# The expert output's running sum: VectorE's add moved to GpSimd, and the copy of the down weights moved ahead in two queues

## The reference, cut to what matters

```
x = x + xattn(layernorm(x), ctx)
h = layernorm(x)
cw = softmax(h @ w_router) * softmax(h @ w_gating / 0.1);  cw /= sum(cw) + 1e-9
for each expert e:  out += cw[:, e] * ((silu(h @ w_gate[e]) * (h @ w_up[e])) @ w_down[e])
x = x + out          # w_gate, w_up: 8 x 256 x 1024; w_down: 8 x 1024 x 256
```

## Time and profile before

| | us |
|---|---|
| median of 3 runs | 963.75 (963.47 to 965.87) |
| the profiled execution, by the device's time | 965.87 |
| its span, first to last instruction | 963.9 |
| PE busy | 959.1 |
| DVE busy | 541.0 |
| ACT busy | 615.3 |
| POOL busy | 642.4 |

### The profile page before, as it was taken

The page is one execution under the profiler, slowest core; times in us unless marked ns, Lnnn a source line. Parts: engine busy times, 40 slices in busy tenths (PEclk is TensorE's granted clock), DMA queues, the critical chain, the costliest instruction groups (busy, mean ns, idle before and its releaser), DMA issues.

```text
span 963.9 us, 14994 instructions
## 1 busy us (share of the span) xinstructions
PE 959.1 (100%) x5090; PEld 890.0 (92%) x5090; DVE 541.0 (56%) x1024; ACT 615.3 (64%) x1109; POOL 642.4 (67%) x536
## 2 busy tenths in 40 slices
PE   9999999999999999999999999999999999999998
PEld 7999899999999999999999999999999999999998
DVE  4998455455555655556555565555555555555564
ACT  6988556666666566666666566666666565666662
POOL 5899975956566665766565675667565656757564
DMA  7462412311001110111010110111100110112035
GB/s 194 141 157 82 126 60 72 112 46 60 23 23 44 42 64 22 45 41 42 23 44 23 42 63 23 45 41 42 45 23 22 43 61 23 45 42 67 14 53 139
DMA packets 73233, 55.85 MB, mean 58 GB/s; under 512 B 30244, under 2 KB 69485, under 8 KB 73158
## 3 DMA queue, kind: packets, MB, share of 16 engines
q1 hardware_dynamic: 73150, 54.91, 19.6%
q10 hardware_dynamic: 8, 0.00, 0.0%
HBM read 46.58 MB, written 6.48 MB: 55 GB/s over the span
## 4 chain that ended last, share of the span: by engine, by line
PE 97%; DVE 1%; DMA 1%; ACT 0%; issue 0%; SPq 0%; DVEq 0%; ACTq 0%
PE ps L355 95%; PE ps L1874 1%; DMA xf<-in_L_xattn_Wk 1%; PE ps L1910 0%; PE ps L1862 0%; PE ps L1927 0%; DVE early L1371 0%; ACT arena L892 0%; DVE xsacc L1562 0%; PE ps L1953 0%; PE ps L1820 0%; ACT xf L900 0%; ACT xf L892 0%; ACT early L879 0%; DVE ps L1553 0%
## 5 line engine op out<-in xcount | busy, mean ns | idle before, releaser
L355 PE MATMUL ps<-arena 128*128 128x448 f32 (+5 forms) x2064 | 388.3, 339 | 0.1
L355 PEld LDWEIGHTS ps<-arena 128*128 128x128 f32 (+2 forms) x2064 | 343.7, 187 | 21.0 <-DVE arena L366 0.4
L702 POOL TENSOR_TENSOR arena<-shared,arena 128x448 fp32r<-128x448 f32 x196 | 223.8, 1160 | 190.7 <-ACT arena L1107 186.8
L355 PE MATMUL ps<-xc_hi,w_hi 128*128 128x448 f32 x904 | 330.8, 366 | 0.1
L355 PE MATMUL ps<-xc_hi,w_lo 128*128 128x448 f32 x904 | 330.2, 365 | 0.0
L355 PE MATMUL ps<-xc_lo,w_hi 128*128 128x448 f32 x904 | 330.2, 365 | 0.0
L355 PEld LDWEIGHTS ps<-xc_hi,w_hi 128*128 128x128 f32 x904 | 169.8, 188 | 14.0 <-DVE ps L1496 0.5
L355 PEld LDWEIGHTS ps<-xc_hi,w_lo 128*128 128x128 f32 x904 | 169.8, 188 | 13.6
L355 PEld LDWEIGHTS ps<-xc_lo,w_hi 128*128 128x128 f32 x904 | 169.9, 188 | 13.1
L1107 ACT CAST arena<-shared 128x448 fp32r<-128x448 f32 x180 | 102.2, 568 | 108.4 <-DVE shared L1521 44.0
L1553 DVE TENSOR_TENSOR ps<-ps,xf 128x448 f32<-128x448 f32 x104 | 65.6, 631 | 146.3 <-PE ps L355 146.3
(11 more groups left out here) (171 smaller groups left out, 1068.1 us busy)
## 6 DMA issues: line engine op xcount, KB each, us to landing
early<-in_L_ffn_w_down SPq DMA_DIRECT2D x16, 512.0 KB, 3.9
xf<-cw_dram SPq DMA_DIRECT2D x16, 448.0 KB, 4.6
shared<-in_ctx SPq DMA_DIRECT2D x16, 336.0 KB
w_raw<-in_L_ffn_w_gate SPq DMA_DIRECT2D x17, 256.0 KB, 2.7
w_raw<-in_L_ffn_w_up SPq DMA_DIRECT2D x17, 256.0 KB, 3.1
early<-in_L_ffn_w_gate SPq DMA_DIRECT2D x15, 256.0 KB, 2.7
early<-in_L_ffn_w_up SPq DMA_DIRECT2D x15, 256.0 KB, 3.1
xsacc<-in_x SPq DMA_DIRECT2D x8, 224.0 KB, 6.1
```

The lines of the kernel that those rows point to most:

```text
L355: ins = nc.tensor.matmul(dst, w, m, start=first and i == 0, stop=last and i == len(passes) - 1, skip_group_check=onto)
L702: nc.gpsimd.tensor_tensor(h[:, 1, j, at:at + TC], tile, h[:, 0, j, at:at + TC].bitcast(fp32), ALU.subtract).then_inc(hid_lo_done, 1)
```

## The change

Groups 4 to 29 get their add from GpSimd. VectorE now multiplies from PSUM into one of two SBUF buffers (`weighed`, two slots of `xf`) and raises `weighed_done`; GpSimd's new `add_unit` adds the buffer to the accumulator and raises `unit_done`. TensorE's units and SP's loads of shares wait for `weighed_done` instead of `unit_done`. VectorE's multiply of unit u waits for GpSimd's add of unit u-2. From set 2 on, `high_down` stands ahead of `gate_seed` on ScalarE, and `low_down` is the first of the quad on GpSimd. In quads 5 and 63 `up_c22` goes behind two `add_rows`.

```diff
+        weighed = [xf[:, 4 + i, :] for i in range(2)]
@@ SP, load_cw
-                    sp.wait_ge(unit_done, UNITS * (HALVES * CP * e - 2 * CP + cp + 1))
+                    sp.wait_ge(weighed_done, UNITS * (HALVES * CP * e - 2 * CP + cp + 1))
@@ GpSimd
+            def add_unit(g, k):
+                if g < 2 * CP:
+                    return
+                u = UNITS * (g - CP) + k
+                pool.wait_ge(weighed_done, u + 1)
+                at_least(pool, unit_done, u - 2 * UNITS * CP + 1)
+                to = unit_at(g, k)
+                nc.gpsimd.tensor_tensor(to, to, weighed[u % 2], ALU.add).then_inc(unit_done, 1)
             def quad(n):
+                if turn == 2 and hn > 1:
+                    low_down(hn)
                 if n > PLAIN:
                     low_hidden(n - 1, HID21, g21, 0, TC)
-                if turn == 2:
-                    low_down(hn)
+                g = n // FPAIRS - 1
+                if n % FPAIRS and g in TURNED:
+                    add_unit(g, 0)
+                    add_unit(g, 1)
+                if n % FPAIRS == 0 and g - 1 in TURNED:
+                    add_unit(g - 1, 3)
...
+                if turn == 2 and hn == 1:
+                    low_down(hn)
                 if turn == 2 and hn + 1 < SETS:
                     sums_of_set(2 * hn + 3)
+                if n % FPAIRS and g in TURNED:
+                    add_unit(g, 2)
...
@@ ScalarE, quad
+                if turn == 2 and hn > 1:
+                    high_down(hn)
                 gate_seed(n)
...
-                if turn == 2:
+                if turn == 2 and hn == 1:
                     high_down(hn)
@@ VectorE, weigh
-                rows, to, share = ps_unit[u % 2], unit_at(g, k), cw_all[:, g % CP, c * TC:(c + 1) * TC]
                 if g < 2 * CP:
                     ve.wait_ge(acc_stored[g % CP], DMA)
-                    nc.vector.tensor_tensor(to, rows, share, ALU.mult).then_inc(unit_done, 1)
+                    to = unit_at(g, k)
                 else:
-                    nc.vector.tensor_tensor(rows, rows, share, ALU.mult).then_inc(weighed_done, 1)
-                    ve.wait_ge(weighed_done, u - UNITS * CP + 1)
-                    ve.wait_ge(unit_done, u - UNITS * CP + 1)
-                    nc.vector.tensor_tensor(to, rows, to, ALU.add).then_inc(unit_done, 1)
+                    at_least(ve, unit_done, u - 2 - UNITS * CP + 1)
+                    to = weighed[u % 2]
+                nc.vector.tensor_tensor(to, ps_unit[u % 2], cw_all[:, g % CP, c * TC:(c + 1) * TC], ALU.mult).then_inc(weighed_done, 1)
@@ VectorE, turn
-                ve.wait_ge(unit_done, UNITS * (len(TURNED) - CP + cp) + k + 1)
+                ve.wait_ge(unit_done, UNITS * (len(TURNED) - 2 * CP + cp) + k + 1)
@@ VectorE, quad
-                up_c22(n)
                 if odd and g not in TURNED:
                     add_rows(g, 2, ps_r[2])
                     add_rows(g, 3, ps_r[3])
+                up_c22(n)
@@ TensorE, unit and down
-                    pe.wait_ge(unit_done, u - 1)
+                    pe.wait_ge(weighed_done, u - 1)
...
-                        pe.wait_ge(unit_done, UNITS * len(TURNED) - 1 + i // 2)
+                        pe.wait_ge(weighed_done, UNITS * len(TURNED) - 1 + i // 2)
```

## The result

The change makes the kernel slower: 970.49 us median over 12 executions (967.51 to 975.98) against 964.01 for the kernel before beside it (963.37 to 965.87). The ratio is 1.0075, 95% interval 1.0053 to 1.0096. The forecast was 964.4 in a range up to 967.2.

What follows compares the result with a forecast made beforehand. The prediction took PE's matmul pace of 0.2026 us as the bound. Its terms, -0.41 + 0.5 + 0.6 = +0.7 us, on the median of 963.75 gave 964.4, in a range of 962.9 to 967.2.

Steps and rivals of the forecast that it cites:

- What bounds the kernel now: Middle of the kernel: PE sets the pace at 0.2026 us a matmul without a gap; no other engine on the path.
- The move of the add: 104 adds leave VectorE (65 us) for GpSimd (1.16 us each, 121 us); adds and both new waits priced at 0.
- SP and TensorE's waits: Shares' loads and TensorE's units wait for the multiply instead of the add, at least 0.6 us earlier; priced at 0.
- Quad 61, -0.41: Weight load behind up_c22 in quad 61: an add ahead of the transposes leaves, so the 0.41 us stall goes.
- `up_c22` behind two `add_rows`, +0.6: Quad 63: up's product 4 loads 0.7 us late, less 0.10 absorbed, +0.6 us; the same exchange in quad 5 costs nothing.
- `high_down` ahead of `gate_seed`, 14 x 0.04 = +0.5: Sets 2 to 15: the large cast delays gate_seed, PE's load is 0.13 us late, 0.03 to 0.04 lost per quad.
- the signs of being wrong: PE waiting for a hidden tile's low part or GpSimd's weights, a changed 0.2026 pitch, or over 0.15 stall per set.
- The bounds: Cost per quad of the cast ahead of gate_seed: from 0 up to 0.24 us, or 3.3 us in all.
- Rival A: Load of the gate's product 6, 14 times: the cast before gate_seed costs much more, up to 967.3 us; chance 0.13.
- B: The new stalls don't come: ScalarE is a little sooner and quad 63 costs half, 963.7 us; chance 0.17.
- C: GpSimd gets late: instructions 20% longer beside VectorE's new SBUF writes delay turn 0's low weights, 967.2 us; chance 0.04.
- D: PE has room: the 7% open in weight-load busy is VectorE interference, giving up to 4.6 us, 959.2; chance 0.02.

Runs made afterwards that it cites:

- The adds alone: Changed kernel with high_down and low_down at their old places and up_c22 ahead of the add_rows again; 963.75 us, a second time 963.93.
- the kernel with the copies back: Changed kernel with high_down and low_down back at their old places, the adds staying on GpSimd; 963.91 us.
- 0.11 late: Kernel before with two ScalarE copies of 448 columns, which nobody reads, ahead of gate_seed in turn 0 of sets 2 to 15; 972.04 us.
- 0.57 late: Kernel before with three ScalarE copies of 448 columns, which nobody reads, ahead of gate_seed in turn 0 of sets 2 to 15; 974.19 us.
- the kernels with even and with odd sets: Kernel before with high_down and low_down moved ahead in the even sets alone, 964.22 us; in the odd sets alone (3 to 15), 972.61 us.
- the move alone: Kernel before with only high_down and low_down moved ahead, the adds staying on VectorE; 970.66 us, on another chip 971.94.

## Why the prediction was wrong, by its own steps

- **What bounds the kernel now**: right. TensorE sets the pace at 0.2026 us, and no other engine is on the path. I took that distance for a constant of the kernel. It is one of two steady paces, and the profile of before shows only the one.
- **The move of the add**: right in its numbers (1155 ns, GpSimd 43.1 of 53.5 us for 43.7) but for one wait that it had at 0, the late load at 518 us. The adds alone give 963.75 and 963.93, no difference from before that these runs can tell. 5 of their 24 executions took 971 to 974 us, which before never did in over 100; that late load stands in both of their profiles, behind a pause of VectorE, and 445 us at the slower pace from there would be 9 us. That this is what happens in those executions is argued and not shown, as none was profiled. The longest, 973.7, is more than that above the others, and the kernel with the copies back has the same late load and no long execution in 11.
- **SP and TensorE's waits**: right, nothing.
- **Quad 61, -0.41**: right; no stall is left there.
- **`up_c22` behind two `add_rows`, +0.6**: right; 0.66 us idle and 0.55 lost.
- **`high_down` ahead of `gate_seed`, 14 x 0.04 = +0.5**: this step failed. Its place and its lateness are right (0.12 us for 0.13), and so is the loss at the load, 0.03 for 0.04. The working stopped there, and took the pace for fixed: of the signs of being wrong that the prediction names, a changed pitch of 0.2026 is the one that came, and it had no price. A late load also leaves TensorE at one pace or the other, and at the slower one each set costs 1.06 us more, until another load is late or TensorE stalls. In the kernel that has this step alone it came to 7.4 us in the long execution that was profiled. No long execution of the changed kernel itself was profiled, so that it runs at the slower pace there too is taken over from that kernel; its 3 to 12 us would be 150 to 600 us of it.
- **The bounds** of that step, 0 to 0.24 per quad, came from neighbouring rows for the length of a wait, and none of them is about what follows a wait.
- **Rival A** named the right place and sign, but its price was 0.1 us per 0.1 of lateness. Measured, 0.11 late and 0.57 late cost nearly the same, and 0.03 at the load stood beside 6 us in all. **B** was out. **C** did not come. **D** is refuted: VectorE works 66 us less, and the pace is 0.2026 as before, with PEld at 92% of the span. The Trainium skill, Perfetto Trace Analysis, Identifying the Most-Contended Engine, judges TensorE's headroom by weight-load busy, beside its share of peak FLOPs; in this trace the open 7% gave nothing back when 66 us of VectorE's work went.

What stays open: why one late load changes the pace and the next, as late to 0.01 us, doesn't; whether the set matters, as the kernels with even and with odd sets ran on different chips; why one chip shows it in most executions of the changed kernel and another in few; and why on that other chip the move alone shows it in most. No kernel here beats before: the best, with the adds alone, stands within its interval.

## What to carry to other kernels

`gate_seed` had 0.8 us of cover before TensorE's weight load, and using it up cost more than the 0.03 us of each late load: before putting work ahead of what releases it, ask what is left, and count a load that gets late at all as a risk for the whole stretch behind it, not at its own 0.03 us. When executions are longer than the profiled one, don't look for bigger gaps only: compare the number of matmuls per window in two stretches, or sum the distances against a kernel without the edit. And look at the single times and not the median alone, since two groups of times point at something that switches.

## What the runs showed that was not expected

- TensorE has two steady paces for the same stream of 448-column matmuls with a load each: 0.2026 us, with starts 0.199 to 0.207 apart, and 0.2067 evenly, both at a granted clock of 1.00. Loads keep up with either (their busy time per set is 49.5 and 49.6 us).
- In these profiles a stream without late loads stays at its pace over hundreds of us: 430 us at the slower one, and the whole middle of before at the fast one.
- VectorE pauses for 0.35 us at fixed places of its program, seven times between 240 and 900 us. Before absorbs them in the cover of `gate_seed`; with that cover gone they cost TensorE 0.2 to 0.4 us each.
